# Moving the 2 KB load of the logits' bias behind the first two loads of the experts on SyncE's queue

## The reference, cut to what matters

```
h       = gelu(cond @ W0 + b0);  h = gelu(h @ W1 + b1)
att     = softmax(h @ W2 + b2)                       # (64, 8)
agg_w   = einsum('bk,koi->boi', att, weight)         # one 32x32 mixing matrix for each sequence
h       = einsum('boi,bih->boh', agg_w, x) + (att @ bias_k)[:, :, None]
routing = sum of the two largest of h @ gate_w
shared  = relu(h @ up_w) ** 2 @ down_w
routed  = ((h @ fc1_w) @ expert_w * routing) @ fc2_w
out     = x + layernorm(shared + routed) * gamma + beta
```

## Time and profile before

| | |
|---|---|
| median of 3 runs | 256.64 us |
| the three runs | 256.37, 256.64, 646.71 us |
| profiled execution, first to last instruction (span) | 254.6 us |
| what the median has above that span | 2.04 us |
| TensorE busy | 248.0 us, 97% of the span |
| mean granted TensorE clock | 0.995 of full speed |
| bytes moved by DMA | 15.60 MB |

### The profile page before, as it was taken

How to read it: one execution, slowest core, us unless ns; L and a number is a source line. 1 busy time by engine, 2 the same in 40 slices (tenths; PEclk the granted TensorE clock), 3 DMA queues, 4 the chain that set the end, 5 groups by cost and what they waited for, 6 DMA issues and landing times.

```text
span 254.6 us, 3526 instructions
## 1 busy us (share of the span) xinstructions
PE 248.0 (97%) x1291; PEld 207.1 (81%) x1291; DVE 155.8 (61%) x272; ACT 81.8 (32%) x142; POOL 39.4 (15%) x45
## 2 busy tenths in 40 slices
PE   8999999999999999999999999999999999999992
PEld 7877887988888888888888888888888888788891
DVE  4798999944448964644447983464444953406453
ACT  4669856411003452321112534331111355202100
POOL 2400021000117120001114411001111700001110
PEclk9999999999999999999999999999999999999997
DMA  6994804001111400001111220000011100000111
GB/s 161 332 324 153 305 17 153 0 0 44 41 41 41 167 0 0 3 0 42 41 41 41 78 87 0 0 0 11 31 41 44 42 0 0 0 3 8 74 44 41
DMA packets 10444, 15.60 MB, mean 61 GB/s; under 512 B 1088, under 2 KB 4928, under 8 KB 10432
## 3 DMA queue, kind: packets, MB, share of 16 engines
q1 hardware_dynamic: 9984, 15.33, 17.6%
q10 hardware_dynamic: 448, 0.11, 0.2%
HBM read 11.23 MB, written 4.20 MB: 61 GB/s over the span
## 4 chain that ended last, share of the span: by engine, by line
PE 89%; DMA 3%; issue 2%; DVE 1%; SPq 1%; ACT 0%; POOL 0%; POOLq 0%; DVEq 0%
PE ps L932 27%; PE ps L934 27%; PE ps L933 27%; PE ps L906 4%; DMA late<-in_up_w_dram 3%; PE ps L998 2%; PE ps L950 1%; PE ps L956 1%; PE ps L952 1%; SPq L322 0%; POOL rstd L417 0%; DVE stats L714 0%; DVE y_buf L712 0%; DVE h_full L636 0%; ACT h_hi L474 0%
## 5 line engine op out<-in xcount | busy, mean ns | idle before, releaser
L932 PE MATMUL ps<-down_hi,sq_hi 128*128 128x512 f32 (+1 forms) x136 | 51.2, 377 | 0.0
L933 PE MATMUL ps<-down_lo,sq_hi 128*128 128x512 f32 (+1 forms) x136 | 51.2, 377 | 0.0
L934 PE MATMUL ps<-down_hi,sq_lo 128*128 128x512 f32 (+1 forms) x136 | 51.2, 376 | 0.0
L932 PE MATMUL ps<-h_hi,up_hi 128*128 128x512 f32 x120 | 46.8, 390 | 0.0
L934 PE MATMUL ps<-h_hi,up_lo 128*128 128x512 f32 x120 | 46.7, 389 | 0.0
L933 PE MATMUL ps<-h_lo,up_hi 128*128 128x512 f32 x120 | 46.7, 389 | 0.0
L417 POOL TENSOR_TENSOR rstd<-mv,half 128x1 f32<-128x1 f32 x16 | 15.3, 954 | 158.2 <-DVE mv L719 153.2
L512 ACT ACTIVATE relu_sq<-ps 128x512 f32<-128x512 f32 x32 | 19.1, 597 | 57.7 <-PE ps L934 44.3
L712 DVE TENSOR_TENSOR y_buf<-ps,y_buf 128x512 f32<-128x512 f32 x15 | 10.4, 692 | 41.0 <-PE ps L934 40.7
L685 DVE CAST sq_hi<-relu_sq 128x512 fp32r<-128x512 f32 x32 | 22.6, 706 | 16.2 <-ACT relu_sq L514 15.7
L932 PEld LDWEIGHTS ps<-down_hi,sq_hi 128*128 128x128 f32 x136 | 25.6, 188 | 4.7
(11 more groups left out here) (137 smaller groups left out, 308.7 us busy)
## 6 DMA issues: line engine op xcount, KB each, us to landing
out_dram<-late SPq DMA_DIRECT2D x15, 256.0 KB, 2.0
x_cur<-in_x_dram SPq DMA_DIRECT2D x3, 1024.0 KB, 5.2
late<-in_down_w_dram SPq DMA_DIRECT2D x4, 512.0 KB, 5.3
late<-in_up_w_dram SPq DMA_DIRECT2D x3, 512.0 KB, 8.8
x_cur<-in_x_dram SPq DMA_DIRECT2D x2, 512.0 KB, 7.2
experts_sb<-in_experts_dram SPq DMA_DIRECT2D x3, 256.0 KB, 3.5
agg_b<-aggb_dram SPq DMA_DIRECT2D x1, 768.0 KB, 4.9
latents_sb<-in_latents_dram SPq DMA_DIRECT2D x1, 528.0 KB, 4.8
```

The costliest lines, as they stand in the source:

```text
L932: nc.tensor.matmul(dst, a_hi, b_hi, start=first, stop=False)
L933: nc.tensor.matmul(dst, a_hi, b_lo, start=False, stop=False)
L934: return nc.tensor.matmul(dst, a_lo, b_hi, start=False, stop=last)
```

## The change: one load, two places later

The load of b2 is issued fourth on SP's queue and no longer second. Nothing else is different: the same 64 pieces of 32 bytes, the same semaphore, the same waits.

```diff
             sp.dma_start(mlp_sb[:, 0:NB + D], mlp[:, 0:NB + D]).then_inc(mlp_loaded[0], 16)
+            for m in range(LC):
+                sp.dma_start(experts_sb[:, m, FIRST], experts_v[:, m, FIRST]).then_inc(experts_loaded[m], 16)
             sp.dma_start(b2_rows[:, :], kernels[0, C * C + C:C * C + C + K].partition_broadcast(NB)
                          ).then_inc(b2_loaded, 16)
-            for m in range(LC):
-                sp.dma_start(experts_sb[:, m, FIRST], experts_v[:, m, FIRST]).then_inc(experts_loaded[m], 16)
             sp.dma_start(experts_sb[:, :, REST], experts_v[:, :, REST]).then_inc(experts_loaded[LC], 16)
```

## The result

| | kernel before | changed kernel |
|---|---|---|
| median | 256.39 us | 257.63 us |
| runs | 14 (256.11 to 258.57, and one of 646.71) | 14 (256.63 to 258.82) |
| span of the profiled execution | 254.6 us | 256.9 us |

The ratio is 1.0045, with a 95% interval of 1.0023 to 1.0067: the change makes the kernel slower, by 1.24 us between the medians. The forecast was 256.4, a gain of 0.2, in a range of 255.9 to 257.4: the measured time lies above that range, and the change has the other sign. The times of the changed kernel lie in two groups of seven: 256.63 to 257.12 (middle 256.73) and 258.15 to 258.82 (middle 258.65). All other kernels are read against runs of the kernel before on the same chip in the same session.

A forecast was written before the change was run, and what follows sets the result against it. TensorE's matmul stream was taken as the bound, so only its start at 15.29 us could move: 0.25 us gained less 0.05 to 0.1 for shared engines, 0.2 net, from 256.64 to 256.4 us, range 255.9 to 257.4.

The forecast's parts named there:

- SP's part: SP's queue in the start-up: same loads in the same total time, issues from line 323 on starting when they did.
- b2 not late: Load of b2, issued at 2.27 us: lands at 5.6 to 5.9, before its need at about 6.2, costing nothing.
- the valley: Low DMA share, 0.70 from 2.50 to 3.75 us against a steady 0.94; the earlier experts' loads would fill it.
- The gain on the queue: SP's loads behind the experts': up_w's first piece lands 0.30 us sooner, at 12.11, bounds nothing and 0.61.
- 0.25 of the 0.30 arrives: From ACT's split to the addition of the bias at 13.69: 0.25 us of the gain gets through.
- The price on ACT's queue: W1, W2 and biases share DMA engines with the experts' first load: condition path 0.1 us late, bounds nothing and 0.55.
- The second rival: ACT's load waits for the whole first experts' load: gelu 0.55 us later, 0.3 lost, time 256.9; chance 0.14.
- The rival on TensorE's clock: Late b2 idles TensorE, clock falls from 2.4 to 1.2 GHz, costing 5.1 us; chance 0.02, shared with anything unnamed.

The follow-up runs named there:

- e4: The kernel before with 2 instead of 4 idle matmuls behind line 866, no load touched: 257.53 us against 256.49.
- e10: The kernel before with no idle matmuls behind line 866: 257.49 us against 256.43.
- e2: The changed kernel with ACT's load of W1, W2 and the biases issued ahead of the mixing weights: 256.57 us against 256.49.
- e5: The changed kernel with ACT's load of W1 ahead of the mixing weights and 6 instead of 4 idle matmuls: 256.85 us against 256.49.
- e7: The kernel before with b2's load moved behind the first experts' load only, the second experts' load behind it: 256.71 us against 256.49.
- e3: The changed kernel with 6 instead of 4 idle matmuls behind line 866: 257.02 us against 256.49.
- e9: The kernel before with ACT's W1 load ahead of the mixing weights and up_w's first piece ahead of the second half of x: 256.52 us against 256.43.
- e8: The changed kernel with SP waiting for DVE's first small reduction before the experts' loads, restoring their old issue time: 256.59 us against 256.49.
- e1: The changed kernel with an unused second copy of the 2 KB load in b2's old place on SP's queue: 257.08 us against 256.49.
- e6: The kernel before with up_w's first piece issued ahead of the second half of x: 256.49 us against 256.49.

## Why the prediction was wrong

- **SP's part was right.** The same issues in the same total time, b2 not late (it landed at 5.5, where the step had 5.6 to 5.9), the valley filled.
- **The gain on the queue was too small, and without effect.** 0.30 us was taken for the first piece of up_w, with 0.61 as the bound; it came 0.97 us sooner (11.44 against 12.41), more than the bound. Nor is this one execution alone: the piece landed at 12.4 to 12.6 in the profiles of the kernel before, e4 and e10, and with the first experts' load early at 11.2 to 11.5 in four (changed kernel, e2, e5, e7), though at 12.2 in e3. Why it is more than the filled valley is open.
- **"0.25 of the 0.30 arrives" failed.** The step checked ACT's copy and DVE's subtraction ahead of line 636, but not PE's line 912, which delivers the mixed x to the same addition. e9 showed it: 0.06 us arrive. This was to be seen in the timeline before, where 20 of these matmuls run from 12.48 on, with the addition at 13.69:

```profile
12.48 2.39 PE L912 MATMUL ps<-mix,x_cur 128*128 128x128 f32 x20
```

- **"The price on ACT's queue" failed, in size.** The step took 0.1 us between bounds of nothing and 0.55. Line 441 was 0.61 late, and 0.41 and 1.23 in the profiles of e7 and e3. The second rival, ACT's load late by all of the experts' first load, was the right one: its landing at 4.43 stands against 4.47 measured. The rival gave 256.9 us, 0.3 over the kernel before; the lower group of the changed kernel lies 0.34 over it (256.73 against 256.39). No execution of that group was profiled, so this agreement is one of times alone. And as an upper bound 4.43 failed: in e3 W1 landed at 5.09. The rule that stood beside it, in the Trainium skill's page "DMA: Bandwidth & Descriptors", section "Queues, rings and completion order", fits the landing at 4.47; no run shows the turns themselves.
- **What made it 1.24 us and not 0.3 was dismissed.** The rival on TensorE's clock saw "no path to so long a gap" and read full clock off the granted clock of the windows. But the start-up runs at the low level up to 6.0 us even in the kernel before, as the durations show, and it does not take a fall: it is enough that the rise comes behind line 859, as it did in the upper execution that was profiled, and by the times in about half of all. e4 brought the upper group without touching a load (5 of 10, against none of 30 in its session), no run of e3 was in it with W1 late and two more idle matmuls (0 of 9), and none of e8 with the experts put back (0 of 12). The last two are set against the 7 of 14 of the changed kernel, which was run in another session. The median of two groups of equal size lies between them; that is the 257.63.

Counted over all sessions, 5 of 93 runs of the kernel before (without that of 646.71) lie above 258 us, against 7 of 14 of the changed one. That the upper group exists in both fits what the Trainium skill says on its page "TensorE: Matmul & The Clock Gate", section "Part 1: The HAM clock gate": the rise varies from run to run of the same kernel. The times fit that; no profile of an upper execution of the kernel before was taken. The traces of this case, which are of different kernels, have the rise anywhere from 4.7 to 10.6 us.

Open is what exactly decides the moment of the rise. e2's slow execution had no wait ahead of line 875, e3's fast one had the second longest, and e10's rise came sooner than the changed kernel's although its gap was longer. Open too is how steady W1's landing is without the change: with the experts at their old time it took 2.3 us after its issue (before and e4), 2.1 (e8 and e10), but 3.0 (e1) and 2.8 (e6) as well; with the experts early 3.3, 3.9 and 3.1 (changed kernel, e3, e7). Each is one execution.

## What to carry to other kernels

A small load at the head of a queue may be worth its place as a spacer: before moving a large load into it, look at what the other queue has in flight then, and how much slack its receiver has. Where work in a start-up is only just in time for TensorE, take into account that its clock may rise late in a part of the executions, read the level off the durations of equal instructions, and look at the single times for groups before the median is read. When several strands meet, list every producer of the meeting instruction before a gain on one of them is counted.

## What the runs showed of the hardware

- The granted clock in the profile read 1.00 in a stretch where passes of one and the same form took nearly twice as long (3.78 against 1.99 us for eight), because the trace has no record of the clock ahead of its first rise (10.5 us in the changed kernel).
- In the twelve profiled executions, all of a start-up that begins work on TensorE at 1.06 us, the clock rose between 4.7 and 10.6 us.
- Two idle matmuls in the start-up, some 0.4 us of TensorE's time together, decided how many executions of a 256 us kernel came 1.6 to 1.9 us late: taken away, 5 of 10 against none of 30 (e4); added to the changed kernel, none of 9, where it had 7 of 14 in another session (e3).
- A 69 KB load on ACT's queue took 2.1 to 3.0 us to its landing when a 256 KB load on SP's queue was issued 0.6 us behind it (six executions), and 3.1 to 3.9 us when both were issued at the same time (three).
- One further 2 KB load on SP's queue delayed a load seven places behind it by 0.8 us (12.41 to 13.21, e1), of which 0.66 us lie in its own later issue.
